# A reciprocal from GpSimd to VectorE, reordered VectorE work, and filler transposes on TensorE

## The chip, the cores and the metric

The kernel runs on one core of a Trainium2 chip. The metric is device time in microseconds for one launch, as the median of several runs.

## The reference

Four sequences of 512 rows with 512 features. First an attention step: scores of a projected 128-wide context with itself, multiplied by the layer norm of x (the row statistics are over 512 features), masked and put through a softmax, which is added to x. Then a mixture of experts on the layer norm of that:

```
shared = silu(x @ shared_gate_w) * (x @ shared_up_w) @ shared_down_w
logits = x @ router_w                       # 8 experts, the best 2 are taken
probs  = sigmoid(top_val) at the chosen two, 0 elsewhere
xin    = probs.T[:, :, None] * x[None]
gate, up = split(einsum('etd,edf->etf', xin, gate_up_w))
out    = shared + sum_e (silu(gate) * up) @ down_w
```

## The kernel before

The 2048 rows are 16 tiles of 128. A first stage of 16 steps does attention, both layer norms and most of the shared expert. Each product is made of three parts (high x high, a bfloat16 correction, low x high), so each tile needs transposes, a high part and a bfloat16 copy by ScalarE (`x_high`, `h_high`), and a low part by VectorE (`x_low`, `h_low`). The order of every engine's work is written out by hand, and the engines meet at semaphores.

Between the first stage and the routed one lies the choice. VectorE finds the best two experts of each row (`choose`), TensorE sums ones and triangles over them (`ranks`), VectorE turns that into a slot for each row (`count`, `place_of_choice`, `job_of_choice`), then builds one-hot matrices in four parts (`row_of_choice`), and TensorE multiplies them (`job_rows`), which gives the table of which row stands at which place of which job. `tables` makes from it the lists `jgather` and `jscatter`, and `scatter_waits` the numbers that scatters have to wait for. Interleaved with this are the last tiles of the shared expert: `gated_shared(14)` and `(15)`, `h_low`, and `y_shared`, which adds the product of `down` to x2. `down(n)` writes the bank `ps_y(n)` and waits until that bank's last reader is through, by the count `y_s`.

The sigmoid of the chosen logits is 1 / (1 + exp(-logit)). ScalarE makes the exponentials (`pexp`), GpSimd the rest into `p8` (lines 409 to 412). SyncE stores p8 behind the normalized rows in `xn_dram` (semaphore `st_p8`), so that a gathered row brings its eight probabilities with it:

```python
pool.wait_ge(p8_s, 1)
g.tensor_tensor(p8[:].rearrange("p t e -> p (t e)"), p8[:].rearrange("p t e -> p (t e)"),
                mone[:].to_broadcast([P, TILES * E]), ALU.pow).then_inc(p8_s, 1)
```

The routed stage has 39 jobs (16 to 54), each of 128 rows for one expert: GpSimd gathers the rows (four jobs ahead), TensorE transposes them, multiplies by gate and up, transposes h, and multiplies by down; GpSimd adds the result to the output with a scattered DMA. On GpSimd the queue is: gathers of jobs 16 to 19 (behind `st_p8` and `table_s`), three low parts of weights, the waits for all y stores, then for each job the gather four ahead and its own scatter. The scatters of the first seven jobs each wait for all before them. TensorE's order for a job is: first gate/up group, h transposes of the job before, the other two groups, x transposes of the next job, down of the job before.

Of the kernel before, what the change touches and what calls it, by code (L numbers as in the profile page):

```python
# [5 lines left out]
P = 128  # L6
B, S, D, H = 4, 512, 512, 128
T = B * S
TILES = T // P
RT = S // P  # L10
KC = D // P
E, K, I = 8, 2, 256
IC = I // P
SHARED = 0
# [20 lines left out]
FIRST = TILES - LAG  # L35


def build(nc, x, ctx, mask, kpad, wq, bq, wk, bk, router_w, gate_up_w, down_w, sg_w, su_w, sd_w, out):
    f32r = mybir.dt.float32r
    f32, bf16, i32, u8 = mybir.dt.float32, mybir.dt.bfloat16, mybir.dt.int32, mybir.dt.uint8  # L40
    ALU, ACT, X = mybir.AluOpType, mybir.ActivationFunctionType, mybir.AxisListType.X
# [7 lines left out]
    with stack:  # L49
# [12 lines left out]
        def new(name, shape, dt=f32):  # L62
            offset = top_of[0]
            top_of[0] = (offset + int(np.prod(shape[1:])) * size[dt] + 31) // 32 * 32
            assert top_of[0] <= nc.sbuf_usable_end
            return at(offset, name, shape, dt)
# [102 lines left out]
        rw_lo = new("rw_lo", [P, KC, E], bf16)  # L169
        bqk = new("bqk", [P, 2])  # L170
        mhalf = new("mhalf", [P, 2])
        mone = new("mone", [P, 1])
        bn = new("bn", [P, XS, 2, 6])
        mv = new("mv", [P, XS, 2, 2])
        ve = new("ve", [P, XS, 2])
# [24 lines left out]
            return bank[0] if n >= TILES - 1 and n % 2 else bank[4]  # L200

        def ps_y(n):
            return bank[1] if n >= TILES and n % 2 or n == TILES - 2 else bank[6]

        def rows_T(n):
            src = ps_xT[n % 2 if n >= TILES else 0]
# [101 lines left out]
        def _(pool):  # L308
# [9 lines left out]
            def iota(dst, pattern, base_, mult):  # L318
# [3 lines left out]
            then(g.memset(ident[:], 0.0))  # L322
            g.affine_select(out=ident[:], in_=ident[:], compare_op=ALU.not_equal, fill=1.0, base=0,
                            pattern=[[-1, P]], channel_multiplier=1).then_inc(c_ident, 1)
            g.memset(mone[:], -1.0)
            g.memset(mhalf[:], -0.5).then_inc(c_half, 1)
            pool.wait_ge(c_half, 1)

# [50 lines left out]
            for s in range(TILES):  # L379
# [22 lines left out]
                if s == 7:  # L402
# [4 lines left out]

            pool.wait_ge(pexp_s, TILES)
            g.tensor_scalar(p8[:], pexp[:], BIG, 1.0, ALU.min, ALU.add).then_inc(p8_s, 1)
            pool.wait_ge(p8_s, 1)  # L410
            g.tensor_tensor(p8[:].rearrange("p t e -> p (t e)"), p8[:].rearrange("p t e -> p (t e)"),
                            mone[:].to_broadcast([P, TILES * E]), ALU.pow).then_inc(p8_s, 1)

            def gather(n):
                r = n % XS
# [197 lines left out]
        def _(dve):  # L613
# [52 lines left out]
            def x_low(n):  # L666
                dve.wait_ge(xbf_s, n + 1)
                if n >= TS:
                    dve.wait_ge(g_ps, n - TS + 1)
                    dve.wait_ge(logit_ps, min(n - TS + 1, TILES))  # L670
                v.tensor_tensor(x_lo[:, n % TS], rows_T(n), x_hi[:, n % TS].bitcast(f32), ALU.subtract).then_inc(xlo_s, 1)  # L671
# [77 lines left out]
            def choose(k, first, end):  # L749
                n = end - first  # L750
                src = lgs[:, first:end, :]
                ids = idx8[:].unsqueeze(1).to_broadcast([P, n, E])
                chosen = oh[:, k].rearrange("p (t e) -> p t e", e=E)[:, first:end, :]
                then(v.tensor_reduce(top[:, k, first:end], src, X, ALU.max))
                then(v.tensor_tensor(eq[:, first:end, :], src, wide(top[:, k, first:end], [P, n, E]), ALU.is_equal))
                then(v.tensor_tensor(eq[:, first:end, :], eq[:, first:end, :], ids, ALU.mult))
                then(v.tensor_reduce(best[:, first:end], eq[:, first:end, :], X, ALU.max))
                then(v.tensor_tensor(chosen, ids, wide(best[:, first:end], [P, n, E]), ALU.is_equal))
                if k == 0:
                    then(v.scalar_tensor_tensor(src, chosen, -BIG, src, ALU.mult, ALU.add))  # L760
# [7 lines left out]
            def last_normal():  # L768
# [4 lines left out]
                v.tensor_scalar(xn[:, t % XS, :], x2[:, t % X2S, :], mv[:, t % XS, 0, 0:1], rstd[:, t % XS, 0:1],  # L773
                                ALU.subtract, ALU.mult).then_inc(xn_s, 1)

            def count():
                dve.wait_ge(rank_ps, 1)
                then(v.tensor_tensor(cmp[:], wide(ps_rank[:, TILES * E:], [P, E, TILES]), k128[:].unsqueeze(1).to_broadcast([P, E, TILES]), ALU.is_gt))
                then(v.tensor_reduce(ntile[0][:, 4:], cmp[:], X, ALU.add))
                for i, d in enumerate((1, 2, 4)):  # L780
                    then(v.tensor_tensor(ntile[i + 1][:, 4:], ntile[i][:, 4:], ntile[i][:, 4 - d:4 - d + E], ALU.add))
                then(v.tensor_tensor(base[:], ntile[3][:, 4:], ntile[0][:, 4:], ALU.subtract))
                then(v.scalar_tensor_tensor(place[:], base[:].unsqueeze(1).to_broadcast([P, TILES, E]), float(P),
                                            ps_rank[:, 0:TILES * E].rearrange("p (t e) -> p t e", e=E), ALU.mult, ALU.add))
# [47 lines left out]
            x_low(TILES - 2)  # L832
            last_normal()
            choose(0, 0, FIRST)
            x_low(TILES - 1)
            choose(1, 0, FIRST)
            fetch(1, FIRST, TILES)
            choose(0, FIRST, TILES)
            choose(1, FIRST, TILES)
            chosen_sum()  # L840
            h_low(FIRST - 1)
            y_shared(FIRST - 2)
            count()
            place_of_choice()
            job_of_choice()
# [4 lines left out]
            job_experts()  # L850
            tables()
            gated_shared(TILES - 2)
            y_shared(FIRST - 1)
            gated_shared(TILES - 1)
            h_low(TILES - 2)
            scatter_waits()
            h_low(TILES - 1)
            y_shared(TILES - 2)
            y_shared(TILES - 1)
# [28 lines left out]
        def _(pe):  # L888
# [81 lines left out]

            def down(n, e):
                pe.wait_ge(hhi_s, n + 1)
                if n == TILES - 2:
                    pe.wait_ge(x2_s, TILES)
                elif n == TILES - 1:
                    pe.wait_ge(y_s, n - 1)
                elif n > TILES + 1:
                    pe.wait_ge(y_s, n - 1)
                elif n:
                    pe.wait_ge(y_s, min(n, TILES))  # L980
                for c in range(IC):
                    tn.matmul(ps_y(n)[:], h_hi[:, n % 2, c, :], dn_hi[:, e, c, :], start=(c == 0), stop=False)  # L982
                pe.wait_ge(hbf_s, n + 1)
                for c in range(IC):
                    tn.matmul(ps_y(n)[:], h_bf[:, n % 2, c, :], dn_lo[:, e, c, :], start=False, stop=False)  # L985
                pe.wait_ge(hlo_s, n + 1)
                for c in range(IC):
                    last = tn.matmul(ps_y(n)[:], h_lo[:, n % 2, c, :], dn_hi[:, e, c, :], start=False, stop=(c == IC - 1))  # L988
                last.then_inc(y_ps, 1)
# [10 lines left out]
            def job_rows(part):  # L1000
                n = NC // 4
                pe.wait_ge(OB_s, part + 1)
                for i in range(part * n, (part + 1) * n):
                    last = tn.matmul(ps_map, OB[part % 2][:, i - part * n, :], R[:, i].rearrange("p m j -> p (m j)"),
                                     start=(i == 0), stop=(i == NC - 1))
                last.then_inc(map_ps, 1)

            pe.wait_ge(c_ident, 1)
            pe.wait_ge(ld_w, 32)
# [37 lines left out]
            logits(TILES - 1)  # L1047
            gate_up_rest(TILES - 2, SHARED)
            gate_up_high(TILES - 1, SHARED)
            gate_up_low(TILES - 1, SHARED)  # L1050
            pe.wait_ge(pexp_s, TILES)
            ranks()
            gate_up_rest(TILES - 1, SHARED)
            down(FIRST - 1, SHARED)
            pe.wait_ge(R1_s, 1)
            for part in range(4):
                pe.wait_ge(R0_s, min(part + 1, 2))
                job_rows(part)
            h_transpose(TILES - 2)
            down(TILES - 2, SHARED)  # L1060
            h_transpose(TILES - 1)
# [58 lines left out]
```

## Time and profile before

| | |
|---|---|
| median of 3 runs | 363.01 us (361.55 to 363.92) |
| the profiled execution | 363.71 us, its span 362.0 us |
| TensorE products busy | 318.5 us, 88% |
| VectorE busy | 210.0 us, 58% |
| ScalarE busy | 177.9 us, 49% |
| GpSimd busy | 230.9 us, 64% |
| mean granted TensorE clock | 0.961 |

All times of the trace are from the start of the span. The 1.7 us between span and time lie around the program. A line number is that of the kernel before.

### The profile page before, as it was taken

The page shows a single profiled execution, that of the slowest core. Times are in us where ns is not written, and L with a number is a line of the kernel's source. Part 1 is how long each engine was busy: PE and PEld are TensorE (multiplying, and loading weights), DVE is VectorE, ACT ScalarE, POOL GpSimd, SP SyncE. Part 2 cuts the span into 40 slices and gives each one's busy share as a digit, 9 for nine tenths or more (in the row PEclk, how much of TensorE's full clock was granted, in tenths as well). Part 3 has the DMA queues.
Part 4 walks back from the last instruction along what each step waited for, and adds up shares of the span by engine and source line. Part 5 has one row for each costly group of instructions (what it writes and reads, how often), then busy time and mean ns, then how long its engine had stood idle before and what let it go on. Part 6 is the DMA issues. An engine that isn't in the chain of part 4 may idle for free.

```text
span 362.0 us, 6464 instructions
## 1 busy us (share of the span) xinstructions
PE 318.5 (88%) x1601; PEld 218.8 (60%) x1627; DVE 210.0 (58%) x461; ACT 177.9 (49%) x400; POOL 230.9 (64%) x199
## 2 busy tenths in 40 slices
PE   2866999999999983628999989999999999999991
PEld 1333666676767762315776757777777777777760
DVE  0766789999998789612444334444444444444441
ACT  2477767757767736102644434444444444444440
POOL 0688999986774749958385554756555465555433
PEclk9989899999999998587999999999999999999997
DMA  7956777857556320075346465867666566675736
GB/s 178 308 197 211 206 228 254 247 194 230 205 162 210 124 89 0 0 199 164 68 82 111 72 116 111 131 113 130 108 116 115 115 120 117 91 133 88 132 36 83
DMA packets 29764, 50.61 MB, mean 140 GB/s; under 512 B 5473, under 2 KB 9313, under 8 KB 29729
## 3 DMA queue, kind: packets, MB, share of 16 engines
q0 software_dynamic: 9008, 21.66, 33.5%
q1 hardware_dynamic: 19232, 27.99, 24.6%
q10 hardware_dynamic: 1488, 0.54, 0.8%
q8 instruction: 16, 0.26, 0.3%
q14 instruction: 20, 0.16, 0.1%
HBM read 30.45 MB, written 19.73 MB: 139 GB/s over the span
## 4 chain that ended last, share of the span: by engine, by line
PE 56%; DMA 11%; issue 11%; POOL 9%; DVE 7%; ACT 4%; POOLq 1%; ACTq 0%; DVEq 0%
PE bank L949 10%; PE bank L959 9%; PE bank L954 9%; DMA out_rows<-y,jscatter 9%; PE bank L982 5%; PE bank L988 5%; PE bank L985 5%; PE bank L1073 4%; PE bank L968 3%; POOL gu_lo L356 2%; PE bank L912 2%; POOL pen L351 2%; DMA kpad_in<-in_mask_BxS_bf 2%; PE bank L921 1%; POOL rstd L332 1%
## 5 line engine op out<-in xcount | busy, mean ns | idle before, releaser
L439 POOL DMA_INDIRECT out_rows<-y,jscatter x39 | 61.9, 1588 | 73.3 <-DMA out_rows<-y,jscatter 47.1
L959 PE MATMUL bank<-gu_hi,x_lo 128*128 (+1 forms) x220 | 70.3, 441 | 0.0
L949 PE MATMUL bank<-gu_hi,x_hi 128*128 (+1 forms) x220 | 63.0, 409 | 3.4 <-POOL dn_lo L356 1.4
L671 DVE TENSOR_TENSOR x_lo<-bank,x_hi 128x512 fp32r<-128x512 f32 x55 | 37.9, 690 | 33.1 <-ACT x_bf L507 33.0
L954 PE MATMUL bank<-gu_lo,x_bf 128*128 (+1 forms) x201 | 54.8, 387 | 1.3 <-issue 0.2
L864 DVE SCALAR_TENSOR_TENSOR h<-bank,xg,h 128x256 f32<-128x256 f32 x39 | 18.9, 484 | 57.8 <-ACT h L595 57.8
L420 POOL DMA_INDIRECT xg<-xn_rows,jgather x39 | 41.7, 1069 | 15.5 <-issue 15.5
L514 ACT CAST h_hi<-bank 128x256 fp32r<-128x256 f32 x55 | 20.6, 375 | 59.6 <-PE bank L968 59.4
L959 PEld LDWEIGHTS bank<-gu_hi,x_lo 128*128 128x128 f32 x220 | 41.7, 190 | 12.8 <-issue 0.6
L356 POOL TENSOR_TENSOR gu_lo<-stage,gu_hi 128x1024 bf16<-128x1024 f32 x18 | 43.3, 2405 | 9.6 <-ACT gu_hi L493 9.6
L949 PEld LDWEIGHTS bank<-gu_hi,x_hi 128*128 128x128 f32 x220 | 41.0, 193 | 13.6 <-issue 3.0
L988 PE MATMUL bank<-dn_hi,h_lo 128*128 (+1 forms) x110 | 45.1, 492 | 0.0
L595 ACT ACTIVATE h<-bank,xg 128x256 f32<-128x256 f32 x39 | 18.5, 474 | 51.8 <-PE bank L959 51.8
L677 DVE TENSOR_TENSOR h_lo<-bank,h_hi 128x256 fp32r<-128x256 f32 x55 | 23.1, 421 | 33.3 <-ACT h_bf L515 33.2
L982 PE MATMUL bank<-dn_hi,h_hi 128*128 (+1 forms) x110 | 38.5, 431 | 1.5 <-ACT h_hi L514 1.5
L506 ACT CAST x_hi<-bank 128x512 fp32r<-128x512 f32 x55 | 32.0, 581 | 15.3 <-PE bank L1073 10.4
L507 ACT CAST x_bf<-bank 128x512 bf16<-128x512 f32 x55 | 32.9, 597 | 0.0
L985 PE MATMUL bank<-dn_lo,h_bf 128*128 (+1 forms) x103 | 32.2, 389 | 0.5
L954 PEld LDWEIGHTS bank<-gu_lo,x_bf 128*128 128x128 bf16 x220 | 20.5, 100 | 18.8 <-issue 5.8
L1073 PE MATMUL bank<-ident,xg 128*128 128x128 f32 x156 | 23.9, 277 | 7.7 <-issue 6.4
L1073 PEld LDWEIGHTS bank<-ident,xg 128*128 128x128 f32 x156 | 19.5, 142 | 13.8 <-issue 6.8
L873 DVE COPY y<-bank 128x512 f32<-128x512 f32 x39 | 26.6, 681 | 1.3 <-PE bank L988 1.3
(128 smaller groups left out, 497.5 us busy)
## 6 DMA issues: line engine op xcount, KB each, us to landing
stage<-in_L_ffn_gate_up_w SPq DMA_DIRECT2D x16, 512.0 KB, 3.8
xin<-in_x SPq DMA_DIRECT2D x16, 256.0 KB, 4.3
xn_rows<-xn SPq DMA_DIRECT2D x16, 256.0 KB, 4.0
stage<-in_L_ffn_down_w SPq DMA_DIRECT2D x8, 512.0 KB, 3.8
out_rows<-x SPq DMA_DIRECT2D x16, 256.0 KB, 4.3
out_rows<-zeros POOLq DMA_DIRECT2D x1, 1024.0 KB, 5.0
ctx_in<-in_ctx SPq DMA_DIRECT2D x1, 768.0 KB, 8.6
xg<-xn_rows,jgather POOLq DMA_INDIRECT x39, 4.3
```

The costliest lines, as they stand in the source:

```text
L356: g.tensor_tensor(third((gu_lo, dn_lo), c), stage[:, c % 3], third((gu_hi, dn_hi), c).bitcast(f32), ALU.subtract).then_inc(lo_s, 1)
L420: g.indirect_dma_start(out=xg[:, r, :], out_offset=None, in_=xn_dram, in_offset=bass.IndirectOffsetOnAxis(ap=jgather[:, n - TILES:n - TILE ...
L439: g.indirect_dma_start(out=out, out_offset=bass.IndirectOffsetOnAxis(ap=jscatter[:, n - TILES:n - TILES + 1], axis=0), in_=y[:, r, :], in_ ...
L507: a.copy(x_bf[:, n % TS], rows_T(n)).then_inc(xbf_s, 1)
L671: v.tensor_tensor(x_lo[:, n % TS], rows_T(n), x_hi[:, n % TS].bitcast(f32), ALU.subtract).then_inc(xlo_s, 1)
L949: tn.matmul(ps_g(n)[:], x_hi[:, n % TS, k, :], gu_hi[:, e, k, :], start=(k == 0), stop=False)
L954: tn.matmul(ps_g(n)[:], x_bf[:, n % TS, k, :], gu_lo[:, e, k, :], start=False, stop=False)
L959: last = tn.matmul(ps_g(n)[:], x_lo[:, n % TS, k, :], gu_hi[:, e, k, :], start=False, stop=(k == KC - 1))
L982: tn.matmul(ps_y(n)[:], h_hi[:, n % 2, c, :], dn_hi[:, e, c, :], start=(c == 0), stop=False)
L985: tn.matmul(ps_y(n)[:], h_bf[:, n % 2, c, :], dn_lo[:, e, c, :], start=False, stop=False)
L988: last = tn.matmul(ps_y(n)[:], h_lo[:, n % 2, c, :], dn_hi[:, e, c, :], start=False, stop=(c == IC - 1))
L1073: last = tn.transpose(ps_xT[n % 2][:, k * P:(k + 1) * P], xg[:, n % XS, k * P:(k + 1) * P], ident[:])
```

## The change

GpSimd no longer raises p8 to the power -1; VectorE takes its reciprocal behind `chosen_sum`. On VectorE `h_low(13)` moves ahead of `x_low(15)`, `y_shared(12)` behind `gated_shared(15)`, and `y_shared(13)` behind `scatter_waits`; the comparisons themselves stay behind `h_low(14)`. The banks of the down products alternate from tile 13 on, and the waits of `down` follow. On TensorE `down(13)` moves ahead of `ranks`, and the low group of tile 15 behind it. `keep_busy` multiplies the identity by itself into bank 2, which nobody reads: 28 times ahead of the job_rows, 4 times behind each of their four parts, and 6 times more at the end.

```diff
--- before.py
+++ after.py
@@ -169,7 +169,6 @@
         rw_lo = new("rw_lo", [P, KC, E], bf16)
         bqk = new("bqk", [P, 2])
         mhalf = new("mhalf", [P, 2])
-        mone = new("mone", [P, 1])
         bn = new("bn", [P, XS, 2, 6])
         mv = new("mv", [P, XS, 2, 2])
         ve = new("ve", [P, XS, 2])
@@ -200,7 +199,7 @@
             return bank[0] if n >= TILES - 1 and n % 2 else bank[4]
 
         def ps_y(n):
-            return bank[1] if n >= TILES and n % 2 or n == TILES - 2 else bank[6]
+            return bank[1] if n >= FIRST - 1 and n % 2 else bank[6]
 
         def rows_T(n):
             src = ps_xT[n % 2 if n >= TILES else 0]
@@ -322,7 +321,6 @@
             then(g.memset(ident[:], 0.0))
             g.affine_select(out=ident[:], in_=ident[:], compare_op=ALU.not_equal, fill=1.0, base=0,
                             pattern=[[-1, P]], channel_multiplier=1).then_inc(c_ident, 1)
-            g.memset(mone[:], -1.0)
             g.memset(mhalf[:], -0.5).then_inc(c_half, 1)
             pool.wait_ge(c_half, 1)
 
@@ -407,9 +405,6 @@
 
             pool.wait_ge(pexp_s, TILES)
             g.tensor_scalar(p8[:], pexp[:], BIG, 1.0, ALU.min, ALU.add).then_inc(p8_s, 1)
-            pool.wait_ge(p8_s, 1)
-            g.tensor_tensor(p8[:].rearrange("p t e -> p (t e)"), p8[:].rearrange("p t e -> p (t e)"),
-                            mone[:].to_broadcast([P, TILES * E]), ALU.pow).then_inc(p8_s, 1)
 
             def gather(n):
                 r = n % XS
@@ -773,6 +768,10 @@
                 v.tensor_scalar(xn[:, t % XS, :], x2[:, t % X2S, :], mv[:, t % XS, 0, 0:1], rstd[:, t % XS, 0:1],
                                 ALU.subtract, ALU.mult).then_inc(xn_s, 1)
 
+            def weights_of_choices():
+                dve.wait_ge(p8_s, 1)
+                v.reciprocal(p8[:], p8[:]).then_inc(p8_s, 1)
+
             def count():
                 dve.wait_ge(rank_ps, 1)
                 then(v.tensor_tensor(cmp[:], wide(ps_rank[:, TILES * E:], [P, E, TILES]), k128[:].unsqueeze(1).to_broadcast([P, E, TILES]), ALU.is_gt))
@@ -832,14 +831,14 @@
             x_low(TILES - 2)
             last_normal()
             choose(0, 0, FIRST)
+            h_low(FIRST - 1)
             x_low(TILES - 1)
             choose(1, 0, FIRST)
             fetch(1, FIRST, TILES)
             choose(0, FIRST, TILES)
             choose(1, FIRST, TILES)
             chosen_sum()
-            h_low(FIRST - 1)
-            y_shared(FIRST - 2)
+            weights_of_choices()
             count()
             place_of_choice()
             job_of_choice()
@@ -850,10 +849,11 @@
             job_experts()
             tables()
             gated_shared(TILES - 2)
-            y_shared(FIRST - 1)
             gated_shared(TILES - 1)
+            y_shared(FIRST - 2)
             h_low(TILES - 2)
             scatter_waits()
+            y_shared(FIRST - 1)
             h_low(TILES - 1)
             y_shared(TILES - 2)
             y_shared(TILES - 1)
@@ -970,14 +970,12 @@
 
             def down(n, e):
                 pe.wait_ge(hhi_s, n + 1)
-                if n == TILES - 2:
+                if n == FIRST - 1:
                     pe.wait_ge(x2_s, TILES)
-                elif n == TILES - 1:
-                    pe.wait_ge(y_s, n - 1)
-                elif n > TILES + 1:
+                elif n >= FIRST:
                     pe.wait_ge(y_s, n - 1)
                 elif n:
-                    pe.wait_ge(y_s, min(n, TILES))
+                    pe.wait_ge(y_s, n)
                 for c in range(IC):
                     tn.matmul(ps_y(n)[:], h_hi[:, n % 2, c, :], dn_hi[:, e, c, :], start=(c == 0), stop=False)
                 pe.wait_ge(hbf_s, n + 1)
@@ -1004,6 +1002,10 @@
                     last = tn.matmul(ps_map, OB[part % 2][:, i - part * n, :], R[:, i].rearrange("p m j -> p (m j)"),
                                      start=(i == 0), stop=(i == NC - 1))
                 last.then_inc(map_ps, 1)
+
+            def keep_busy(count):
+                for _ in range(count):
+                    tn.transpose(bank[2][:, 0:P], ident[:], ident[:])
 
             pe.wait_ge(c_ident, 1)
             pe.wait_ge(ld_w, 32)
@@ -1047,15 +1049,18 @@
             logits(TILES - 1)
             gate_up_rest(TILES - 2, SHARED)
             gate_up_high(TILES - 1, SHARED)
-            gate_up_low(TILES - 1, SHARED)
+            down(FIRST - 1, SHARED)
             pe.wait_ge(pexp_s, TILES)
             ranks()
+            gate_up_low(TILES - 1, SHARED)
             gate_up_rest(TILES - 1, SHARED)
-            down(FIRST - 1, SHARED)
+            keep_busy(28)
             pe.wait_ge(R1_s, 1)
             for part in range(4):
                 pe.wait_ge(R0_s, min(part + 1, 2))
                 job_rows(part)
+                keep_busy(4)
+            keep_busy(6)
             h_transpose(TILES - 2)
             down(TILES - 2, SHARED)
             h_transpose(TILES - 1)
```

## Rows read from the trace of the kernel before

**Rows 1.** Busy time by stage: stretch, length, busy us of each engine, PEclk, DMA.
```profile
141.90:148.20 6.30, 2.49 (x32) 1.91 (x32) 6.06 (x15) 1.98 (x8) 6.30 (x1) 0.58 0.00 0
...
260.00:280.00 20.00, 19.90 (x102) 14.26 (x103) 9.00 (x17) 9.15 (x22) 11.32 (x10) 1.00 0.61 107
```

**Rows 2.** The chain that ended last: start us, us, what, number of instructions.
```profile
152.34 0.44 PE bank L968 x2
...
154.87 6.36 issue
161.23 1.10 PE bank L1073 x4
...
163.29 2.07 PE bank L949 x4
...
167.90 0.44 PE bank L1073 x4
...
333.09 0.93 PE bank L949 x4
...
337.84 0.93 PE bank L949 x4
```

**Rows 3.** Timeline of TensorE's products, 135 to 170 us, with idle time before.
```profile
135.06 0.22 PE L997 MATMUL bank<-ohs,triangle 128*128 128x136 bf16 x1
...
141.92 0.46 PE L1004 MATMUL bank<-R,OB 128*128 128x78 bf16 x8 [4.29 <-DVE OB L807]
...
143.05 0.68 PE L1004 MATMUL bank<-R,OB 128*128 128x78 bf16 x8 [0.68 <-DVE OB L807]
...
149.38 1.22 PE L982 MATMUL bank<-dn_hi,h_hi 128*128 128x512 f32 x2 [0.46 <-ACT h_hi L514]
...
169.20 1.18 PE L949 MATMUL bank<-gu_hi,x_hi 128*128 x4 [0.87 <-issue]
```

**Rows 4.** Timeline of GpSimd, 132 to 184 us.
```profile
132.58 20.76 POOL L411 TENSOR_TENSOR p<-p,mone 128x128 f32<-128x128 f32 x1
...
157.41 1.24 POOL L420 DMA_INDIRECT xg<-xn_rows,jgather  x1 [4.07 <-issue]
...
176.16 1.64 POOL L439 DMA_INDIRECT out_rows<-y,jscatter  x1 [5.11 <-DVE y L873]
...
181.97 1.59 POOL L439 DMA_INDIRECT out_rows<-y,jscatter  x1 [2.77 <-DMA out_rows<-y,jscatter]
```

**Rows 5.** DMA issues, 150 to 215 us: KB, median us to landing.
```profile
xn_rows<-p SPq DMA_DIRECT2D x1, 64.0 KB, 3.0
```

**Rows 6.** Timeline of VectorE, 129 to 149 us.
```profile
129.13 0.69 DVE L671 TENSOR_TENSOR x_lo<-bank,x_hi 128x512 fp32r<-128x512 f32 x1 [0.19 <-ACT x_bf L507]
...
134.11 0.28 DVE L766 TENSOR_TENSOR ohs<-oh 128x128 bf16<-128x128 f32 x1
...
135.31 0.29 DVE L778 TENSOR_TENSOR cmp<-bank,k 128x128 f32<-128x128 f32 x1
...
140.56 4.62 DVE L807 TENSOR_TENSOR OB<-iotap,rowf 128x1024 bf16<-128x1024 bf16 x4
...
146.64 0.18 DVE L826 TENSOR_SCALAR jgather<-tok 128x39 int32<-128x39 f32 x1
...
147.30 0.41 DVE L682 SCALAR_TENSOR_TENSOR h<-h,bank 128x256 f32<-128x256 f32 x1
...
148.09 0.68 DVE L691 TENSOR_TENSOR x<-bank,x 128x512 f32<-128x512 f32 x1
```

**Rows 7.** The reciprocal of one element, by its tile: ns min/median/max.
```profile
L655 DVE RECIPROCAL rinv<-rowsum x16: 129/164/165, 17.9 to 122.3; 128x1 f32<-128x1 f32 x16
```

**Rows 8.** Waits, 160 to 362 us: engine waited for, us in total, times, longest.
```profile
PE bank L1073 <- DMA xg<-xn_rows,jgather: 1.4, 2, 0.8
```

**Rows 9.** Busy time in two slices of 1 us, as in rows 1.
```profile
36.00:37.00 1.00, 0.96 (x11) 0.88 (x8) 0.28 (x2) 1.00 (x3) 1.00 (x1) 1.00 0.99 365
37.00:38.00 1.00, 1.00 (x2) 0.83 (x3) 0.53 (x1) 1.00 (x4) 0.95 (x1) 0.52 0.33 125
```

## Prediction

> **What bounds the kernel now.** I read the 40 slices first: TensorE is at nine tenths from about 163 us to the end, with a hole between 137 and 163 us. Then the stages by window. In the routed stage TensorE is busy 19.90 of 20.00 us at a granted clock of 1.00, and two jobs in a row begin their first product 4.75 us apart (333.09 and 337.84) [rows 1, 2]. So from job 17 on TensorE is the bound, and whatever moves job 17 earlier moves the end by as much, unless the scatter chain on GpSimd objects (below). Job 17's first product starts at 169.20 [rows 3]. The question is what holds it there.
>
> Going back along the chain: TensorE ends the last shared down projection at 154.87, then there are 6.36 us that the chain can only call "issue", then job 16's transposes at 161.23 [rows 2]. "Issue" means only that the profile sees no releaser. The code has one: the gather waits for `st_p8`, the store of the sigmoids. GpSimd's own rows show it: the `pow` of line 411 runs from 132.58 for 20.76 us, to 153.34 [rows 4]; the store of p8 lands 3.0 us after its issue [rows 5]; the first gather starts at 157.41 [rows 4]. The list of rows, `jgather`, which the gather also needs, is ready at 146.64 + 0.18 = 146.82 [rows 6]. So `pow`, store and gather end last, by some ten microseconds over the tables, and by six over TensorE's own work.
>
> Second, the clock. TensorE is at 0.58 on the mean of 141.9 to 148.2 [rows 1], and at 163.29 four products take 2.07 us that take 0.93 us at 337.84: the low level again, 1.2 of 2.4 GHz [rows 2]. Before the first fall it sat idle 4.29 us, before the second 6.36 us [rows 2, 3].
>
> **The reciprocal.** Removed: 20.76 us of `pow`. Left on GpSimd: the min/add of line 409, just ahead. Added on VectorE: one reciprocal over 128 elements in each partition, behind `chosen_sum`. No row shows that form. The nearest are the reciprocal of one element, 0.16 us, and the pass over 128x128 in float32, 0.29 us [rows 6, 7]; several passes for each element cannot be excluded, so I take 0.3 us and bound it by 0.13 and 1.1 us (four passes). It is covered: `ohs` leaves VectorE at 134.11 + 0.28 = 134.39, TensorE needs until 135.06 + 0.22 = 135.28 for the ranks, and `count` starts at 135.31 [rows 3, 6]. 0.9 us of cover; above that, each further tenth shows. The wait for `p8_s` is met, since the `pow` could begin at 132.58 [rows 4]. The same SyncE queue holds the store of p8 ahead of four y stores; it now lands near 138.5, and costs nothing.
>
> The Trainium skill ("VectorE: DVE Perf Modes", its section on the eight slices) says that Reciprocal uses an iterative divide with a repeat count of 8. Were that eight cycles for each element it would be an estimated 1.1 us at the 0.96 GHz of the page "Trainium Architecture — The Big Picture", and `count` would be 0.2 us later; no row here shows it.
>
> **The moves on VectorE.** `h_low(13)` now stands ahead of `x_low(15)`, which started at 129.13 after 0.19 us of idleness [rows 6]. 0.4 us of work in 0.19 us of idleness makes x_low, logits 15, the second choice and `ohs` about 0.2 us late. At `count` the two passes that went (`h_low(13)`, `y_shared(12)`, together 1.0 us) give nothing back, because the ranks end last there: the ranks come at 135.3 + 0.2. From there to the tables VectorE has no idle time (the four OB passes are back to back from 140.56 for 4.62 us [rows 6]), so `jgather` (146.64 [rows 6]) is ready at 147.0. The gather then needs what it needed before, from its start to job 16's transposes 161.23 - 157.41 = 3.8 us [rows 3, 4]: data at about 151. In the diff the scatter comparisons are not put directly behind the tables: they stay behind `h_low(14)`, and only `y_shared(13)` changes sides. Six short passes, 1.1 us.
>
> **What ends last then.** TensorE's shared tail. Its start hangs on VectorE: gated_shared(14) at 147.30 [rows 6] + 0.2, two passes of together 0.87 us (it ended at 148.17 before), so h transposes at 148.4; from there to the first down product it was 149.38 - 148.17 = 1.2 us at the low clock [rows 3], so that could be at 149.6, at full clock 149.2. But `down(14)` now goes to bank 6 and waits for `y_s` 13, that is y_shared(12), which stands behind gated_shared(15): 148.4 + 0.87 + 0.68 = 149.9. This new wait costs 0.3 to 0.7 us; queued behind it on TensorE are h_transpose(15), down(15) and the x transposes of job 16. In exchange `down(15)` goes to bank 1 and waits for y_shared(13), at 149.9 + h_low 0.34 + comparisons 1.1 + 0.68 = 152.0, no later than its h_hi. At full clock a product is 0.93 / 4 = 0.23 us and a down projection six of them, 1.4 us: down(14) ends 151.3, transposes and h_hi until 152.1, down(15) from 152.2 to 153.5. At the low clock all along it would be down(14) 2.8 and transposes and h_hi 1.2, with down(15) at 153.9 and the clock back as it was then: about 155.3. Middle, with the clock lost for a part: 154.2. The gather (151) is hidden by 2.5 us or more. Term one: 161.23 - 154.2 = 7.0 us, bounds 5.9 and 7.7.
>
> **Job 16.** From its transposes to job 17's first product it took 169.20 - 161.23 = 7.97 us with the low clock for most of it [rows 2, 3]. At full clock: from the transposes to the first product 163.29 - 161.23 = 2.06 less 0.44 for four faster transposes, 1.62; three groups of four products, which are a steady job less its down, x and h transposes, 4.75 - 1.4 - 0.44 - 0.22 = 2.7; transposes 0.44; and 169.20 - 168.34 = 0.86 until the next x_hi: 5.6 us, or 2.3 us less. The 6.36 us of idleness ahead of it are gone, so the low clock has lost its reason; a remnant may stay. Term two: 2.1 us, bounds 0 and 2.3.
>
> **The transposes as filler.** Two transposes take 0.44 us at the low clock (152.34) and four take 0.44 us at the full one (167.90) [rows 2]: 0.22 and 0.11 us each. 28 at full clock are 3.1 us, from about 137.3 (ranks 135.5, then the low and rest products 1.8 us) to 140.4; the first OB is not ready before 142. 28 at the low clock would be 6.2 us and reach 143.5, over the cover by 1.4 us. Each four between the job_rows are 0.44 us in a period of 1.155 us of which job_rows took 0.46 at full clock and 0.68 at the low one [rows 3, 6]: covered at full clock (0.90), not at the low one (1.56). The last ten end by 147, or by 149.7 at the low clock. They cost nothing if the clock is kept.
>
> **Sum.** 7.0 + 2.1 = 9.1 us. The profiled execution took 363.71 us for a span of 362.0, so 354.6; it lies 0.7 above the median of the runs, which gives 353.9 from the median. I say 354.2.
>
> **Does the start of the routed stage follow?** GpSimd's four gathers and three low parts move by 157.41 - 147.2 = 10.2 us. It then waited 5.11 us for y of job 16 before its first scatter [rows 4], and keeps nearly that. The wait of TensorE for gathers, 1.4 us in two places [rows 8], comes from the first scatters, each of which waits for the landing of the one before, and moves along unchanged.
>
> **Rivals.**
>
> (a) The filler doesn't hold the clock. For it: in the slice from 36 to 37 us TensorE's records are busy 0.96 us, with transposes and eight-column products, and yet the clock falls to 0.52 in the next [rows 9]; light work did not keep it there. Against it: a slice is not a proof, and the fillers leave no pause over 2 us until 147, where the idle time before the fall was 4.29 us [rows 3]. Then job_rows with their fillers take 4 x 1.56 us from 142.1, behind part three at 147.5 rather than 146.0: tables 1.2 us later than 146.8. down(14) starts at 151.1 at the low clock, 2.7 + 0.7 + 0.4 + about 2.2 gives job 16 at 157.2, and job 17 at 162.9: gain 6.3 us, 357.
>
> The Trainium skill ("TensorE: Matmul & The Clock Gate", Part 4: PE-mode transpose) says that transposes in that mode don't count as busy for the clock. By that rule rival (a) is the outcome. The rows leave it open: they time the transposes (0.22 and 0.11 us, in step with the clock [rows 2]) but don't say what counts.
>
> (b) Everything holds and the clock never falls: job 16 at 153.5, term two 2.3: gain 10.0, 353.3.
>
> (c) The gathers, now issued while three y stores leave on SyncE, land late and end last. Each microsecond over 2.5 costs one; a landing stretched by half as much again stays hidden, twice as much costs 1.3 us: 355.5.
>
> (d) Slower than before: the scatter chain. Its early links go from 176.16 to 181.97 [rows 4], 5.8 us, against 4.75 us for a job; TensorE already meets it with nothing to spare (1.4 us of waits [rows 8]), so every further microsecond in one of the seven links passes through to the end. If the earlier start puts other transfers among them and a link grows beyond 5.8 + 9.1 / 7 = 7.1 us, the gain is gone; at 8 us for a link it is 7 x 2.2 = 15.4 - 9.1 = 6.3 us slower, 370. Against it: the y stores have landed by 159, before the first scatter at 166, and the low parts among the links are the same two.
>
> **How the numbers follow.** The forecast with its neighbours (b, and a clock lost only in the pause at 147 to 150): 0.58. (a) 0.27, (c) 0.08, (d) 0.03, anything that I don't see 0.04. Differences under 1% (3.6 us) are about what a measurement of this kernel can't tell. All but (d) and part of the unseen are over 1% faster: 0.93; within 1% 0.04; slower 0.03. The range goes from the full gain, 353.3 less 1.2 us for the scatter of the runs, to (a) with the same on top: 352.0 to 358.2.
>
> **What would show it.** Right: line 411 gone, gather at 147 on GpSimd, job 16's transposes at 153.5 to 155 with no idle six microseconds, job_rows at 1.00 of the clock, all four groups near 0.46 us; job 17 at 159 to 161; 4.75 us for a job as before. Wrong: tables later than 147.3 (reciprocal or fillers in the way); granted clock 0.5 between 141 and 148 in spite of the fillers (a); TensorE waiting for gathers more than 1.4 us in all (c, d). The forecast fails as a whole if another wait stood behind `st_p8` that the rows don't show.

## The result, and the profile after

The changed kernel took 354.98 us (median of 4 runs, 354.75 to 355.12) beside 363.02 us for the kernel before (4 runs, 361.55 to 363.92): a ratio of 0.9776, with a 95% interval of 0.9755 to 0.9798. 354.2 was forecast. In three more comparisons the ratio was 0.9765, 0.9760 and 0.9756. The profiled execution took 354.75 us for a span of 353.0, 8.96 us less than the profiled one of before.

First the work that gave the wait its length. GpSimd's timeline of the changed kernel, where [rows 4] showed 20.76 us of `pow`:

```profile
131.93 0.68 POOL L407 TENSOR_SCALAR p<-pexp 128x128 f32<-128x128 f32 x1 [6.84 <-ACT pexp L514]
148.13 1.24 POOL L415 DMA_INDIRECT xg<-xn_rows,jgather  x1 [15.53 <-DVE jgather L825]
...
166.79 1.64 POOL L434 DMA_INDIRECT out_rows<-y,jscatter  x1 [5.11 <-DVE y L873]
...
172.59 1.59 POOL L434 DMA_INDIRECT out_rows<-y,jscatter  x1 [2.77 <-DMA out_rows<-y,jscatter]
```

Nothing lies between the min/add and the first gather, and the gather's 15.53 us of idleness now end with `jgather`. The gather starts at 148.13 where it started at 157.41. The wait before the first scatter is 5.11 us as before: GpSimd moved along with TensorE. Nothing of the job 16 idleness is left on TensorE (products of the changed kernel, in order of time; line 1008 are the fillers, 1078 the x transposes):

```profile
134.92 0.22 PE L995 MATMUL bank<-ohs,triangle 128*128 128x136 bf16 x1
...
136.76 3.22 PE L1008 MATMUL bank<-ident 128*128 128x128 f32 x28
141.77 0.46 PE L1002 MATMUL bank<-R,OB 128*128 128x78 bf16 x8 [1.80 <-DVE OB L806]
...
144.27 0.73 PE L1002 MATMUL bank<-R,OB 128*128 128x78 bf16 x8
...
150.00 0.70 PE L980 MATMUL bank<-dn_hi,h_hi 128*128 128x512 f32 x2 [1.03 <-DVE x L686]
...
153.77 0.60 PE L1078 MATMUL bank<-ident,xg 128*128 128x128 f32 x4
155.52 1.18 PE L949 MATMUL bank<-gu_hi,x_hi 128*128 x4 [1.15 <-ACT x_hi L501]
...
159.81 1.20 PE L949 MATMUL bank<-gu_hi,x_hi 128*128 x4 [0.87 <-issue]
```

Job 16's transposes come at 153.77, directly behind the last shared down product, where [rows 2] has 161.23. The 28 fillers take 3.22 us, then there are 1.80 us of pause, and from the second group on the job_rows take 0.68 to 0.73 us: the clock fell there in spite of the fillers. By windows (columns as in [rows 1]):

```profile
140.00:142.50 2.50, 0.73 (x12) 0.71 (x12) 2.50 (x3) 2.50 (x17) 0.00 (x0) 1.00 0.00 0
143.00:146.00 3.00, 3.00 (x29) 2.88 (x29) 2.93 (x5) 0.51 (x1) 0.00 (x0) 0.50 0.02 5
147.00:153.00 6.00, 3.52 (x18) 1.99 (x17) 5.04 (x19) 1.29 (x4) 3.95 (x4) 1.00 0.39 110
153.00:160.00 7.00, 4.98 (x26) 3.32 (x24) 2.43 (x4) 2.42 (x5) 6.97 (x4) 1.00 0.93 301
260.00:280.00 20.00, 20.00 (x104) 14.39 (x103) 8.79 (x16) 8.77 (x22) 10.32 (x9) 1.00 0.65 118
```

It is at the low level from 143 to 146 and back at the full one from 147, with idle time on both sides; before, down(14) still ran at the low one at 149.38 [rows 3]. In the routed stage nothing changed, 20 us busy of 20. On VectorE, the rows that answer to [rows 6, 7]:

```profile
133.97 0.28 DVE L761 TENSOR_TENSOR ohs<-oh 128x128 bf16<-128x128 f32 x1
...
134.17 0.95 DVE L773 RECIPROCAL p<-p 128x128 f32<-128x128 f32 x1
135.17 0.29 DVE L777 TENSOR_TENSOR cmp<-bank,k 128x128 f32<-128x128 f32 x1
...
146.71 0.20 DVE L824 TENSOR_TENSOR tok<-amap 128x39 f32<-128x39 f32 x1 [0.35 <-ACT amap L584]
146.94 0.18 DVE L825 TENSOR_SCALAR jgather<-tok 128x39 int32<-128x39 f32 x1
...
149.18 0.68 DVE L686 TENSOR_TENSOR x<-bank,x 128x512 f32<-128x512 f32 x1
```

The reciprocal of 128 elements takes 0.95 us and `count` starts directly behind it at 135.17, 0.14 us earlier than before. `jgather` is 0.3 us later (146.94 for 146.64), since VectorE waits 0.35 us for the table: the job_rows behind fillers at the low clock come later than VectorE now.

**A common starting point.** The stage ahead of the choice ends at another time in each execution: the last normal on VectorE (`xn` of tile 15) starts anywhere from 125.6 to 126.8 us, in whichever kernel. So I measure from there; the expectations below call it the 15th normal. The table gives, for each profiled execution, the time from this `xn` to `jgather`, to the first product of down(14), to job 16's transposes and to job 17's first product, and then the time from job 17 to the end of the span; last the median of the runs and the median of before beside it.

| kernel | jgather | down(14) | job 16 | job 17 | job 17 to end | median us | before us |
|---|---|---|---|---|---|---|---|
| before | 19.96 | 22.70 | 34.55 | 42.52 | 192.80 | | 363.02 |
| changed | 20.32 | 23.38 | 27.15 | 33.19 | 193.19 | 354.98 | 363.02 |
| after_again | 20.28 | 23.34 | 27.11 | 32.86 | 192.37 | 353.27 | 362.03 |
| after_3 | 19.90 | 22.96 | 28.24 | 33.97 | 192.50 | 354.72 | 363.20 |
| after_4 | 20.30 | 23.36 | 28.65 | 34.37 | 192.65 | 354.13 | 363.05 |
| recip_only | 20.44 | 23.17 | 28.49 | 34.42 | 192.04 | 354.89 | 362.03 |
| all_but_recip | 20.14 | 23.20 | 34.51 | 42.06 | 191.72 | 362.21 | 362.03 |
| no_filler | 19.90 | 22.96 | 28.25 | 34.16 | 191.94 | 353.00 | 362.03 |
| no_filler_2 | 19.89 | 22.95 | 28.67 | 34.40 | 192.93 | 354.85 | 363.20 |
| bridge | 19.89 | 22.96 | 28.04 | 33.76 | 192.55 | 354.30 | 363.20 |
| y_first | 19.90 | 22.38 | 27.52 | 33.25 | 192.83 | 353.55 | 363.20 |
| y_first_no_filler | 19.88 | 22.61 | 28.30 | 34.03 | 192.68 | 354.80 | 363.05 |
| hold | 19.89 | 22.38 | 26.18 | 31.90 | 192.78 | 352.43 | 363.05 |
| slow_links_2 | 19.88 | 22.93 | 28.01 | 33.74 | 197.46 | 359.50 | 363.33 |

Two things are to be seen before any experiment is told. The time from job 17 to the end varies by 1.5 us (191.72 to 193.19) among kernels that differ in nothing there, so differences of some tenths in the medians can't be told from it. And the changed kernel itself reaches job 17 at four different times, 32.86 to 34.37.

### The profile page after: what moved, and what is told of

It is laid out like the page before. It is cut to its first block, busy times and chain, and to the rows that moved or that the text cites. A ratio compares the mean times of both kernels' runs of the same rounds, so it can differ in the third digit from the quotient of the medians.

```text
span 353.0 us, 6588 instructions
## 1 busy us (share of the span) xinstructions
PE 323.0 (91%) x1677; PEld 224.1 (63%) x1677; DVE 210.4 (60%) x462; ACT 178.0 (50%) x400; POOL 210.2 (60%) x197
## 4 chain that ended last, share of the span: by engine, by line
PE 66%; POOL 9%; DMA 7%; issue 7%; DVE 5%; ACT 3%; POOLq 0%; ACTq 0%; DVEq 0%
PE bank L949 12%; PE bank L959 11%; PE bank L954 11%; PE bank L980 6%; PE bank L986 6%; PE bank L983 6%; PE bank L1078 4%; DMA out_rows<-y,jscatter 4%; PE bank L968 3%; POOL gu_lo L354 3%; PE bank L912 2%; POOL pen L349 2%; DMA kpad_in<-in_mask_BxS_bf 2%; PE bank L937 1%; PE bank L935 1%
## 5 line engine op out<-in xcount | busy, mean ns | idle before, releaser
L954 PE MATMUL bank<-gu_lo,x_bf 128*128 (+1 forms) x220 | 57.5, 385 | 0.0
L672 DVE TENSOR_TENSOR h_lo<-bank,h_hi 128x256 fp32r<-128x256 f32 x55 | 23.1, 420 | 31.7 <-ACT h_bf L510 31.7
L983 PE MATMUL bank<-dn_lo,h_bf 128*128 (+1 forms) x110 | 33.3, 385 | 0.0
L986 PEld LDWEIGHTS bank<-dn_hi,h_lo 128*128 128x128 f32 x110 | 20.8, 190 | 8.2 <-DVE h_lo L672 0.4
L354 POOL TENSOR_TENSOR dn_lo<-stage,dn_hi 128x1024 bf16<-128x1024 f32 x9 | 21.9, 2433 | 5.4 <-ACT dn_hi L488 5.3
```

Source lines behind the costliest of these rows:

```text
L354: g.tensor_tensor(third((gu_lo, dn_lo), c), stage[:, c % 3], third((gu_hi, dn_hi), c).bitcast(f32), ALU.subtract).then_inc(lo_s, 1)
L954: tn.matmul(ps_g(n)[:], x_bf[:, n % TS, k, :], gu_lo[:, e, k, :], start=False, stop=False)
```

## The experiments

**1. The reciprocal alone** (recip_only): the kernel before, `pow` and `mone` gone, one line in VectorE's order.

```diff
             chosen_sum()
+            weights_of_choices()
             h_low(FIRST - 1)
```

> The kernel before with one edit: the reciprocal on VectorE behind chosen_sum in place of the pow. No moves, no fillers. My theory (pow, store and gather held job 16): the reciprocal's 0.95 us stands ahead of the count and makes the tables 0.9 us later (147.7), TensorE's shared tail ends near 155.7, job 16's transposes follow at once near 155.7, job 17 near 161.8; the time is 356 to 357 us. Rival (the moves and fillers carry the gain): within 2 us of 363.

354.89 us beside 362.03, ratio 0.9814 (0.9782 to 0.9846). Products on TensorE:

```profile
149.81 1.22 PE L982 MATMUL bank<-dn_hi,h_hi 128*128 128x512 f32 x2 [0.46 <-ACT h_hi L509]
...
155.13 0.60 PE L1073 MATMUL bank<-ident,xg 128*128 128x128 f32 x4
...
161.06 1.19 PE L949 MATMUL bank<-gu_hi,x_hi 128*128 x4 [0.87 <-POOL gu_lo L354]
```

Job 16's transposes at 155.13, job 17 at 161.06 (the expectation had 155.7 and 161.8, and a time of 356 to 357 us; 354.89 is below that). The store of the sigmoids behind `pow` was the wait, and this one edit gives 7.1 of the 8.8 us that the whole change gives in the same comparison. Against the common starting point it brings job 17 8.10 us forward, where the four profiles of the changed kernel have 8.15 to 9.66. Down(14) still runs at the low clock (1.22 us for two products). Although it does, job 17 follows job 16's transposes by 5.93 us, not 7.97: term two of the forecast comes with the idleness gone, with no filler at all. Experiment 2 is the other side of it: with 7.39 us of idleness left, it is 168.68 - 161.13 = 7.55 us.

**2. Everything but the reciprocal** (all_but_recip): the changed kernel, sigmoids by `pow` on GpSimd as before.

```diff
+            pool.wait_ge(p8_s, 1)
+            g.tensor_tensor(p8[:].rearrange("p t e -> p (t e)"), p8[:].rearrange("p t e -> p (t e)"),
+                            mone[:].to_broadcast([P, TILES * E]), ALU.pow).then_inc(p8_s, 1)
...
-            weights_of_choices()
```

> The changed kernel with the pow back on GpSimd: moves, banks and fillers stay. Theory: job 16's transposes stay at 161.2 +- 0.3 and the time at 362 to 364 us, since everything else ends ahead of the gather. Rival: the moves and fillers are worth something alone, 358 to 361 us.

362.21 us beside 362.03, ratio 1.0004 (0.9984 to 1.0025). On TensorE:

```profile
145.44 0.46 PE L1002 MATMUL bank<-R,OB 128*128 128x78 bf16 x8 [0.22 <-DVE OB L807]
...
152.12 0.73 PE L980 MATMUL bank<-dn_hi,h_hi 128*128 128x512 f32 x2 [0.46 <-ACT h_hi L514]
...
161.13 1.08 PE L1078 MATMUL bank<-ident,xg 128*128 128x128 f32 x4 [7.39 <-issue]
```

The clock held here through all job_rows (0.46 us) and both down projections, as it does at the job_rows in some executions of the changed kernel too (experiment 3); TensorE was through early, and then it stood idle for 7.39 us. Faster work ahead of a wait that ends elsewhere buys nothing. The rival that the moves carry the gain is out.

**3. Without fillers** (no_filler, no_filler_2):

```diff
-            keep_busy(28)
...
-                keep_busy(4)
-            keep_busy(6)
```

> The changed kernel without any of the 54 filler transposes. Theory: the low clock lasts from 143 to about 153 instead of 3.5 us, the table lists are 0.2 to 0.3 us earlier (146.7), down(14) starts at 149.8 at the low clock, job 16's transposes at 155.2, job 17 at 161; 1.2 to 1.5 us slower than the changed kernel, 356.3. Rival (fillers are worth nothing, or cost as much as they give): 354.7 to 355.2.

> The kernel without fillers once more. Theory: job 17 again 34.2 us after the 15th normal (1.0 to 1.3 later than with fillers), and the time, with its late gathers at jobs 22 to 26 like those of the others, 0.5 to 1.2 us above the changed kernel in the same call. Rival (the routed stage gives the fillers' gain back by later gathers): the same time within 0.3 us, with 192.0 us or less from job 17 to the end against 192.4 or more for the changed kernel.

The changed kernel has 28 + 4 x 4 + 6 = 50 fillers, not 54. Without them it took 353.00 us in the comparison in which the changed kernel had 353.27, and 354.85 in the one in which it had 354.72. In the trace job 17 comes at 34.16 and 34.40, against 32.86, 33.19, 33.97 and 34.37 with fillers: 0.7 us on the mean, overlapping, and in the medians nothing that can be told. My expectations, 1.2 to 1.5 us and then 0.5 to 1.2 us, were not met (no_filler was 0.27 us below the changed kernel and no_filler_2 0.13 above). The rival, that the routed stage gives the gain back, wanted 192.0 us or less from job 17 to the end: 191.94 in the first trace, 192.93 in the second, so it is not shown either. The two kernels also say what the moves and banks are worth beside the reciprocal: `jgather` comes at 19.90 for 20.44 in recip_only, but job 17 at 34.16 and 34.40 for 34.42, which is nothing that can be told. The repeats of the changed kernel (after_again, after_3, after_4) say why.

> The changed kernel once more, beside the others on the same chip: 354.7 to 355.3 us, job 17 at 159.8. If the phase of the clock matters, the profile's low stretch near 143 to 146 lies elsewhere and the time moves by up to 1 us.

> The changed kernel a third time, as the partner of the other three. Theory: job 17 at 32.9 to 33.2 us after the 15th normal. From job 17 to the end 192.0 to 193.2 us, the difference lying in the gathers of jobs 22 to 27 that come late.

> The changed kernel a fourth time, as the partner of these three: job 17 at 32.9 to 34.0 us after the 15th normal, as the low spell falls beside the down products or on them; before minus after 8.0 to 9.0 us.

The medians were 353.27, 354.72 and 354.13. The first is below what I expected, beside a kernel before that was 1.0 us faster too (362.03 for 363.02). Job 17 came at 32.86, 33.97 and 34.37 us: the second and the third lie outside my 32.9 to 33.2 and 32.9 to 34.0. The granted clock of after_4, in steps of 3 us (stretch, length, TensorE busy, PEclk):

```profile
140.00:143.00 3.00, 1.94 (x23) 0.84 0.00 0
143.00:146.00 3.00, 3.00 (x29) 0.59 0.02 5
146.00:149.00 3.00, 1.08 (x8) 0.98 0.00 0
149.00:152.00 3.00, 2.96 (x8) 0.50 0.84 232
152.00:155.00 3.00, 2.47 (x12) 0.95 0.90 295
```

Here it fell twice: once at the job_rows, and again from 149 to 152, on down(14), behind the pause that the fillers leave from 147 on (1.08 us busy of 3). In the first profile of the changed kernel only the first fall happened, and the down products ran at full clock; in after_3 only the second, at down(14). Where down(14) keeps the full clock, job 17 comes at 32.86 and 33.19, 1.0 to 1.5 us ahead of the kernel without fillers; where it doesn't, at 33.97 and 34.37, between 0.4 us ahead of it and 0.2 us behind. Which of the two an execution gets differs from one to the next with the same code.

**4. The pause of 1.8 us closed** (bridge): `keep_busy(43)` in place of `keep_busy(28)`.

> The changed kernel with 43 fillers ahead of the job_rows in place of 28, which closes the pause of 1.8 us there. Theory: the clock never falls between 137 and 147, the four job_rows take 0.46 us each, the table lists come 0.35 us earlier against the 15th normal (20.0 in place of 20.3 us after it), and job 17 0.3 to 0.4 us earlier (32.6 us after it). In the time 0.3 us, near what can't be told. Rival (transposes don't count for the clock): it falls near 142 as before, job 17 at 33 us or later after the 15th normal.

```profile
135.85 4.86 PE L1008 MATMUL bank<-ident 128*128 128x128 f32 x43
...
144.26 0.46 PE L1002 MATMUL bank<-R,OB 128*128 128x78 bf16 x8 [0.22 <-DVE OB L806]
...
149.49 1.41 PE L986 MATMUL bank<-dn_hi,h_lo 128*128 128x512 f32 x2
```

The first half is as expected: fillers until 140.7, all job_rows at 0.46 us, `jgather` at 19.89. The second isn't: two products of down(14) take 1.41 us, the clock fell in the midst of it, and job 17 comes at 33.76, not 32.6. The time, 354.30, is 0.4 us under the changed kernel of the same comparison, which can't be told from nothing.

**5. The new wait of down(14)** (y_first, y_first_no_filler): `y_shared` ahead of what doesn't hurry.

```diff
             gated_shared(TILES - 2)
+            y_shared(FIRST - 2)
             gated_shared(TILES - 1)
-            y_shared(FIRST - 2)
             h_low(TILES - 2)
+            y_shared(FIRST - 1)
             scatter_waits()
-            y_shared(FIRST - 1)
             h_low(TILES - 1)
```

> The changed kernel with y_shared(12) ahead of gated_shared(15), and y_shared(13) ahead of scatter_waits. Theory (down(14)'s new wait for y_shared(12) costs 0.6 us on the path): down(14) starts 22.7 to 22.8 us after the 15th normal in place of 23.35, job 17 at 32.3 to 32.6; 0.6 us faster. Rival (the gather ends last, not TensorE's tail): down(14) earlier, job 16's transposes unchanged at 27.1.

> y_first without any filler. Theory: down(14) 22.4 us after the 15th normal at the low clock, job 16 at 27.7 to 28.0, job 17 at 33.5 to 33.8, and the time within 0.5 us of y_first: fillers that stop at 147 buy at most what the phase of the fall happens to leave.

Down(14) starts at 22.38, where 22.7 to 22.8 was expected. After_3 has the same `jgather` (19.90) and a fall at down(14) too, and there it starts at 22.96: the order is worth 0.6 us, as expected. Job 16 moves with it (27.52 for 28.24), so TensorE's tail and not the gather ended last. Job 17 comes at 33.25, not at 32.3 to 32.6: the clock fell on down(14) here too. Without fillers down(14) starts at 22.61, job 16 comes at 28.30 and job 17 at 34.03, each 0.2 to 0.3 us over what I expected. The medians are 353.55 beside 354.72 for the changed kernel, and without fillers 354.80 beside 354.13 (ratios to before 0.9733 and 0.9773, with intervals that overlap); neither pair is clear of its scatter by itself. I had expected the two within 0.5 us of each other; the ratios put 1.4 us between them, with the same uncertainty.

**6. Fillers in every pause** (hold): y_first, and

```diff
-            keep_busy(28)
+            keep_busy(43)
...
-            keep_busy(6)
+            keep_busy(17)
             h_transpose(TILES - 2)
+            keep_busy(5)
             down(TILES - 2, SHARED)
             h_transpose(TILES - 1)
+            keep_busy(5)
             down(TILES - 1, SHARED)
...
             x_transpose(TILES)
+            keep_busy(8, 3)
```

The second argument is the bank, 2 where there is none.

> y_first with fillers in every pause: 43 ahead of the job_rows, 17 more at the end of them, 5 behind each shared h transpose, 8 (into bank 3) behind job 16's x transposes. Theory: the granted clock stays at 1.00 from 137 us into the routed stage, down(14) starts 22.4 us after the 15th normal and both downs take 1.4 us, job 16's transposes at 26.0 (or when its rows land), job 17 at 31.7: 1.5 us ahead of y_first's profile, and the time 0.5 to 1.5 us below y_first. Rival (the gather's landing is next): job 16 not before 26.8. Rival (only heavy products keep the clock): it falls in spite of the fillers.

352.43 us (351.83 to 353.22) beside 354.13 for the changed kernel and 363.05 for the one before, ratio 0.9708 (0.9682 to 0.9734). The clock by windows, and three rows of TensorE:

```profile
140.00:143.00 3.00, 2.74 (x29) 1.00 0.03 5
143.00:146.00 3.00, 2.45 (x35) 1.00 0.00 0
146.00:149.00 3.00, 2.87 (x26) 1.00 0.00 0
149.00:152.00 3.00, 3.00 (x18) 1.00 0.68 179
152.00:155.00 3.00, 3.00 (x21) 1.00 0.93 267
```

```profile
149.20 0.73 PE L980 MATMUL bank<-dn_hi,h_hi 128*128 128x512 f32 x2
...
153.00 0.60 PE L1080 MATMUL bank<-ident,xg 128*128 128x128 f32 x4
...
158.72 1.19 PE L949 MATMUL bank<-gu_hi,x_hi 128*128 x4 [0.87 <-POOL dn_lo L354]
```

PEclk is 1.00 in all of it. Job 16 at 26.18 and job 17 at 31.90, where 26.0 and 31.7 were expected: 1.0 us ahead of the earliest profile of the changed kernel, 2.5 ahead of the latest. The time is 1.7 us below the changed kernel of the same comparison, whose ratio is 0.9756 (0.9724 to 0.9789), so the intervals just meet. Against y_first, by the ratios, it is 0.9 us, inside the 0.5 to 1.5 us expected. This is the fastest version here by the median and by the trace.

**7. Slower links in the scatter chain** (slow_links_2): three small steps on GpSimd, on a tile that is no longer read, ahead of the scatters of jobs 17 to 22.

```diff
+                if first and n > TILES:
+                    for _ in range(3):
+                        then(g.memset(pexp[:], 0.0))
                 g.indirect_dma_start(
```

> The changed kernel with three small memsets of a dead tile on GpSimd, each waiting for the one before, between the wait and the issue of the scatters of jobs 17 to 22: an estimated 0.3 us each from other short steps on that engine, so about 0.9 us for a link and 5 us in all over six links. Theory (from job 17 on TensorE and the scatter chain bound together, and the late gathers of jobs 23 to 27 already cost 1 to 2.5 us): 3 to 5 us slower than the changed kernel, in jobs 22 to 27. Rival (TensorE alone is the bound and the chain has slack): under 1 us.

359.50 us beside 363.33 for the kernel before, a gain of 3.8 us where the changed kernel's four comparisons have 8.0 to 8.9. So the memsets cost 4.2 to 5.1 us (3 to 5 were expected), and the trace has 197.46 us from job 17 to the end in place of 192.4 to 193.2. GpSimd, and two of the x transposes on TensorE:

```profile
199.12 0.73 POOL L436 MEMSET pexp<- 128x128 f32 x3 [1.86 <-issue]
200.69 1.59 POOL L437 DMA_INDIRECT out_rows<-y,jscatter  x1 [0.85 <-DVE h L867]
...
205.49 0.72 POOL L436 MEMSET pexp<- 128x128 f32 x3 [1.83 <-issue]
207.05 1.59 POOL L437 DMA_INDIRECT out_rows<-y,jscatter  x1 [0.83 <-DVE h L867]
```

```profile
200.56 0.66 PE L1081 MATMUL bank<-ident,xg 128*128 128x128 f32 x4 [1.50 <-DMA xg<-xn_rows,jgather]
...
206.90 0.66 PE L1081 MATMUL bank<-ident,xg 128*128 128x128 f32 x4 [1.37 <-DMA xg<-xn_rows,jgather]
```

The link from scatter to scatter is 6.4 us here. Over the six links, from the scatter of job 16 to that of job 22, it is 207.05 - 167.11 = 39.94 us where the changed kernel takes 201.61 - 166.79 = 34.82: 5.1 us more, and the end comes 4.3 to 5.1 us later. TensorE waits up to 1.50 us for a gather, where the changed kernel's waits are 0.6 and 0.8 us:

```profile
202.26 0.66 PE L1078 MATMUL bank<-ident,xg 128*128 128x128 f32 x4 [0.61 <-DMA xg<-xn_rows,jgather]
...
207.99 0.66 PE L1078 MATMUL bank<-ident,xg 128*128 128x128 f32 x4 [0.76 <-DMA xg<-xn_rows,jgather]
```

So the chain has hardly any slack: what was added to it came out at the end. This is the place and the price of rival (d), which did not come about in the changed kernel: its first link is 172.59 - 166.79 = 5.80 us. (The prediction counted seven links; the seven scatters have six.)

## Why the prediction was right

**The bound and the wait.** Right, and shown by experiments 1 and 2: the reciprocal alone moves job 16 by six microseconds, everything else alone by nothing.

**The reciprocal's price.** I took 0.3 us and bounded it by 1.1; it is 0.95, three times what I took and near the bound. The cover of 0.9 us took it nearly whole: it ends at 134.17 + 0.95 = 135.12, the ranks at 134.92 + 0.22 = 135.14, and `count` starts at 135.17. Where there was no such room, in recip_only, the tables came 0.5 us later.

**Term one**, 7.0 us with bounds 5.9 and 7.7: 161.23 - 153.77 = 7.46, and from the common starting point 7.40, 7.44, 6.31 and 5.90 in the four profiles, all within the bounds, the last at the lower one. The new wait of down(14) for y_shared(12) is there and costs what was said (150.00; y_shared(12) 149.18 to 149.86).

**Term two**, 2.1 us: 7.97 - (159.81 - 153.77) = 1.93, and 2.2 in the other three profiles. Its reason was the right one of the two given: recip_only has it (5.93) with no filler.

**What failed** is the weight given to the fillers. The prediction said that they "cost nothing if the clock is kept", named a clock of 1.00 at all four job_rows as a sign of being right, and made of a clock that isn't kept rival (a), at 6.3 us of gain. The sign of (a) is what came: PEclk 0.50 from 143 to 146. In the four profiles of the changed kernel the clock fell at the job_rows in three and at down(14) in two, and was kept throughout in none; but the price of (a) was too high. With the fillers at the low clock `jgather` comes 0.4 us later than without them (20.32 for 19.90), not 1.2: the first group still ran at the full clock, and those behind it start 1.36 and 1.42 us apart (142.91, 144.27, 145.69), where (a) had four times 1.56. The fall at down(14) costs 1.5 us (from there to job 16 3.77 us in the first profile, 5.28 us in after_3). After_4, with both, has job 17 at 34.37, a gain of 8.15 us and not 6.3. So the forecast, which took the clock as lost for a part, was near for the sum, but 9.1 us lies in the middle of 8.15 to 9.66 us that one and the same kernel gives, and that the first profile (9.33) was near it is in part luck.

**The end.** Job 17 was 9.39 us earlier and the span only 9.0 shorter: 193.19 - 192.80 = 0.39 us went into the routed stage, 0.27 of it between job 22 and job 27, well inside the 1.5 us by which that stretch varies. TensorE's waits for gathers did not grow (0.61 + 0.76 us, 1.4 as before), so what took it stays open. The rest of the distance to 354.2, some tenths, is no more than the comparisons differ by: the four comparisons give gains of 8.0, 8.8, 8.5 and 8.9 us.

**Rival (c)**, late gathers of job 16: no. Experiment 6 pulled TensorE's tail 0.9 us ahead of the changed kernel's best (26.18 for 27.11) and the gather still did not end last.

## What to carry to other kernels

Where the chain says "issue", read in the code what the next instruction waits for, and look for the long step of another engine that ends just ahead of it; one costly operation (`pow` on GpSimd 20.76 us, the reciprocal on VectorE 0.95) can be the whole gap. On GpSimd it is the operation that is dear: the min/add over the same 128x128 took 0.68 us, and `pow` over two elements in each partition (line 332) 0.71. What `pow` would take on VectorE, or a reciprocal on GpSimd, no run shows. Filler work that keeps TensorE's clock was worth something reliable here only where it reached to the last pause ahead of the products that need the clock (experiment 6). And when an execution differs from the next by more than an edit is worth, compare from the last common event, not from the start.

## What the runs showed that I had not expected

**Transposes hold the clock, and raise it.** In hold TensorE does little from 137 to 149 us but transposes of the identity and the job_rows, and PEclk stays at 1.00 (experiment 6). In the changed kernel, after the fall, it rose again at about 146 in the midst of them (0.50 from 143 to 146, 1.00 from 147), where without fillers it stayed low through the same job_rows:

```profile
140.00:143.00 3.00, 1.36 (x16) 0.50 0.00 0
143.00:146.00 3.00, 1.36 (x16) 0.50 0.00 0
146.00:149.00 3.00, 1.12 (x3) 0.50 0.15 26
149.00:152.00 3.00, 2.91 (x8) 0.51 0.83 262
```

The Trainium skill ("TensorE: Matmul & The Clock Gate", Part 4: PE-mode transpose) says that transposes in that mode don't count as busy for the clock. Whether these are in that mode the trace doesn't say; as this kernel issues them, they count, and the measurement decides.

**A VectorE pass that starts with the `pow` is longer.** The masking of the two last tiles' best logits (128x16, line 760 before) took 0.42 us in both kernels with `pow`, in which it began within 0.01 us of it, and 0.17 or 0.18 us in those without (here the changed kernel). Likewise the VectorE pass that begins within 0.1 us behind GpSimd's min/add took 0.26 us, and the same pass 0.17 or 0.18 us the next time. That the two engines get in each other's way is my reading; no run isolates it. Without `pow` these 0.25 us are gone, which is about what `h_low(13)` cost on VectorE. The first two rows are of all_but_recip, the last of the changed kernel.

```profile
132.69 20.77 POOL L411 TENSOR_TENSOR p<-p,mone 128x128 f32<-128x128 f32 x1
...
132.70 0.42 DVE L760 SCALAR_TENSOR_TENSOR lgs<-oh,lgs 128x16 f32<-128x16 f32 x1
```

```profile
132.70 0.17 DVE L755 SCALAR_TENSOR_TENSOR lgs<-oh,lgs 128x16 f32<-128x16 f32 x1
```
